# Independent work set between the steps of VectorE's dependent chains, two small steps given to ScalarE, and the two convolution tiles in turn

## The reference

```python
# block 1, a selective state-space layer (512 channels, 16 states)
xb, z = split(rms_norm(x) @ in_proj_w)            # 512 + 512
xc = silu(causal_depthwise_conv(xb, 4 taps) + conv_b)
dt, B, C = split(xc @ x_proj_w, [1, 17])
dt = softplus(dt @ dt_proj_w + dt_proj_b)
h_t = exp(dt_t * A) * h_(t-1) + dt_t * B_t * xc_t # for each channel and state
y_t = sum over states of h_t * C_t
y = (y + xc * D) * silu(z) @ out_proj_w + residual
# block 2, a mixture of 16 experts (256 -> 128 -> 256)
scores = sigmoid(x @ gate_weight.T)               # + e_bias for the choice only
# 2 of 4 groups by their two best scores, then the 4 best experts within them,
# weights = the chosen scores over their sum
y = sum over experts of weight * (silu(x @ Wg) * (x @ Wu)) @ Wd
```

## Time and profile before

| | |
|---|---|
| median of 3 runs | 2573.94 us (2572.68 to 2574.6) |
| the profiled execution | 2572.43 us, span 2570.6 us |
| busy of the span: PE, DVE, ACT, POOL | 92%, 92%, 62%, 58% |
| granted TensorE clock, mean | 0.971 |
| steady passes | 2 to 13, about 150 us each |

### The profile page before, as it was taken

One profiled execution on the slowest core, in us unless ns is written; L12 is line 12 of the kernel. 1 busy time (PEld: TensorE's weight loads), 2 busy tenths in 40 slices (PEclk: granted clock), 3 DMA queues, 4 the chain that ended last, 5 costly groups with the idle time before them and its releaser, 6 DMA issues.

```text
span 2570.6 us, 26578 instructions
## 1 busy us (share of the span) xinstructions
PE 2361.5 (92%) x8416; PEld 1172.0 (46%) x8416; DVE 2375.5 (92%) x2831; ACT 1602.5 (62%) x3186; POOL 1494.2 (58%) x531
## 2 busy tenths in 40 slices
PE   6556899999999999999999999999999999988998
PEld 2112354544545454454545445454544545443555
DVE  4989999999999999999999999999999999999642
ACT  6566567666766667676676667666666766654341
POOL 0555556657566665756666575656657566666522
PEclk9778899999999999999999999999999999998999
DMA  4442433535353453534344353534535353443232
GB/s 151 168 147 77 152 117 131 169 98 187 114 161 120 137 172 100 185 114 156 124 142 167 98 186 116 163 117 139 170 100 184 116 158 114 143 157 93 76 77 63
DMA packets 172919, 344.48 MB, mean 134 GB/s; under 512 B 16075, under 2 KB 81388, under 8 KB 164460
## 3 DMA queue, kind: packets, MB, share of 16 engines
q1 hardware_dynamic: 164860, 334.93, 39.0%
q0 software_dynamic: 7920, 7.87, 2.3%
HBM read 291.35 MB, written 51.38 MB: 133 GB/s over the span
## 4 chain that ended last, share of the span: by engine, by line
DVE 63%; issue 18%; PE 10%; ACT 8%; DMA 0%; POOL 0%; DVEq 0%; ACTq 0%; POOLq 0%
DVE hs L1085 30%; DVE hs L1065 14%; DVE th L1185 5%; DVE th L1180 5%; PE MY L511 2%; PE Gp L493 2%; PE Up L501 2%; DVE XC L1027 2%; ACT dA L604 1%; ACT SZ L677 1%; DVE SZ L1092 1%; ACT L604 1%; DVE DX L1049 1%; ACT L677 1%; PE FP L418 1%
## 5 line engine op out<-in xcount | busy, mean ns | idle before, releaser
L947 POOL TENSOR_TENSOR hs<-hs,Cb 128x2048 f32<-128x2048 f32 x256 | 1159.2, 4528 | 160.3 <-DVE hs L1065 159.7
L604 ACT ACTIVATE dA<-dtr,A 128x512 f32<-128x512 f32 x1024 | 700.8, 689 | 732.8 <-DVE hs L1085 730.3
L932 POOL TENSOR_TENSOR th<-th,cmb 128x512 f32<-128x512 f32 x256 | 325.8, 1275 | 899.5 <-DVE hs L1065 805.0
L1085 DVE TENSOR_TENSOR_SCAN hs<-dA,carry,hs 128x512 f32<-128x512 f32 x512 | 626.7, 1264 | 5.9 <-ACT dA L604 5.5
L1085 DVE TENSOR_TENSOR_SCAN hs<-dA,hs 128x512 f32<-128x512 f32 x512 | 595.0, 1202 | 14.2 <-ACT dA L604 13.7
L1065 DVE TENSOR_TENSOR hs<-dxr,Bb 128x2048 f32<-128x2048 f32 x255 | 586.1, 2298 | 1.6 <-PE Y L527 1.6
L493 PE MATMUL Gp<-x2T,Wgu 128*128 128x512 f32 x1024 | 510.5, 621 | 24.8 <-DVE th L1180 24.1
L511 PE MATMUL MY<-Wdn,th 128*128 128x256 f32 x2048 | 485.9, 381 | 0.8 <-POOL th L932 0.8
L501 PE MATMUL Up<-x2T,Wgu 128*128 128x512 f32 x1024 | 482.5, 593 | 0.0
L511 PEld LDWEIGHTS MY<-Wdn,th 128*128 128x128 f32 x2048 | 383.4, 190 | 136.2 <-issue 92.8
L493 PEld LDWEIGHTS Gp<-x2T,Wgu 128*128 128x128 f32 x1024 | 177.1, 191 | 353.4 <-issue 277.6
(11 more groups left out here) (180 smaller groups left out, 1754.0 us busy)
## 6 DMA issues: line engine op xcount, KB each, us to landing
dxr<-dx_d SPq DMA_DIRECT2D x128, 512.0 KB, 7.1
cmb<-cm_d SPq DMA_DIRECT2D x256, 256.0 KB, 3.6
dtr<-dt_d SPq DMA_DIRECT2D x63, 1024.0 KB, 5.5
Wdn<-in_w_dn SPq DMA_DIRECT2D x256, 128.0 KB, 3.4
Bb<-bc_d SPq DMA_DIRECT2D x64, 256.0 KB, 3.0
Cb<-bc_d SPq DMA_DIRECT2D x64, 256.0 KB, 3.4
dt_d<-XB SPq DMA_DIRECT2D x15, 1024.0 KB, 4.3
dx_d<-DX SPq DMA_DIRECT2D x15, 1024.0 KB, 5.8
```

The costliest lines, as they stand in the source:

```text
L604: act.activation(dA[h % 2][:, :], dtr[:, M % 2, beta, :], ACT.Exp, scale=A[:, k:k + 1]).then_inc(s_dA, 1)
L932: pool.tensor_tensor(th[:, q % NTH, :], th[:, q % NTH, :], cmb[:, q % 2, :], ALU.mult).then_inc(m_a, 1)
L947: pool.tensor_tensor(hs[:, G % NH, :, :], hs[:, G % NH, :, :], Cb[:, s, :].unsqueeze(1).broadcast_to([P, NBETA, CH]), ALU.mult).then_inc(s ...
L1085: dve.tensor_tensor_scan(hv, dA[h % 2][:, :], hv, first, ALU.mult, ALU.add).then_inc(s_h, 1)
```

## The change

Five things are changed.

1. `inputs` can be issued in parts, by 4 (512 columns each) or by 8 (256 columns each). In group 4 the four parts are set into `newton` of `norms`, after its steps guess, t0, y0 and t1; in group 6 likewise in `p_scale2`; in group 9 of passes with `R_` eight parts are set into the routing. The `inputs` at the end of these groups goes. `s_u` is raised by the last part, and the wait on `s_y` is before the first.
2. In group 9, `y_out` stands behind the routing's first instruction and no longer behind its last.
3. The variance of `p_scale2` (step `Bw1`) is now an activation of ScalarE (`var2`), and `comb` is now written by four activations of ScalarE (`p_comb`, behind `f_softplus` in group 9). The factor 0.5 moves into the copy `cmT`.
4. The two convolution tiles are both done in group 3, tap by tap in turn: tile 0, tile 1, tile 0, and so on; none is done in group 2.
5. In group 12 ScalarE issues `tanh` before two of the `decay` and not behind them.

```diff
@@ -184,12 +184,12 @@
             ['xT0', 'xT1', 'raw0', 'tap0', 'raw1', 'tap1', 'raw2', 'raw3', 'tap2', 'tap3', 'silu_x', 'z0', 'xd', 'dt', 'z1', 'z2', 'z3', 'silu_z'])
-        f_dve = Steps(sem('f_dve'), [f'c{k}{m}' for m in DVE_CONV for k in range(HIST)] + ['hist', 'dx'])
+        f_dve = Steps(sem('f_dve'), [f'c{k}{m}' for k in range(HIST) for m in DVE_CONV] + ['hist', 'dx'])
         fp_full = sem('fp_full')
         s_u, s_dA, s_h, s_keep, s_c, s_y, y_gate = (sem(k) for k in ('s_u', 's_dA', 's_h', 's_keep', 's_c', 's_y', 'y_gate'))
-        route = ['score', 'sfc', 'ps', 'hs', 'gs', 'geq', 'ggt', 'gq', 'gr', 'tmp', 'top', 'le', 'eq', 'nle', 'cs', 'ok', 'oke', 'sel', 'w', 'ws', 'wr', 'comb']
-        p_dve = Steps(sem('p_dve'), ['Bw1'] + rsqrt_names('q') + ['Bnb'] + route)
-        p_act = Steps(sem('p_act'), ['xn0', 'xn1', 'rev0', 'nm0', 'rev1', 'nm1', 'sq', 'ro', 'sq2', 'x2', 'x2T0', 'x2T1', 'ex', 'sig', 'cmT'])
+        route = ['score', 'sfc', 'ps', 'hs', 'gs', 'geq', 'ggt', 'gq', 'gr', 'tmp', 'top', 'le', 'eq', 'nle', 'cs', 'ok', 'oke', 'sel', 'w', 'ws', 'wr']
+        p_dve = Steps(sem('p_dve'), rsqrt_names('q') + ['Bnb'] + route)
+        p_act = Steps(sem('p_act'), ['xn0', 'xn1', 'rev0', 'nm0', 'rev1', 'nm1', 'sq', 'ro', 'sq2', 'var2', 'x2', 'x2T0', 'x2T1', 'ex', 'sig', 'comb', 'cmT'])
         m_g, m_u, m_d, m_th, m_v, m_w, m_a = (sem(k) for k in ('m_g', 'm_u', 'm_d', 'm_th', 'm_v', 'm_w', 'm_a'))
...
         z_dve = Steps(sem('z_dve'), ['w1'] + rsqrt_names('r') + ['nb'])
@@ -478,7 +478,7 @@
                 bank_free(p, 'ct')
-                pe.wait_ge(p_dve.sem, p_dve.at(c, 'comb'))
+                pe.wait_ge(p_act.sem, p_act.at(c, 'comb'))
                 for b in range(TB):
...
                 mm.then_inc(fp_full, 1)
@@ -729,6 +729,8 @@
                 squares(x1[:, (p - 1) % 2, :, :], b_s, n_nm[:, (p - 1) % 4, TB:2 * TB], dx_half).then_inc(p_act.sem, 1)
+                act.wait_ge(p_act.sem, p_act.at(p - 1, 'sq2'))
+                act.activation(p_w[:, 0, :], b_s[:, :], ACT.Copy, scale=1.0 / DM, bias=LN_EPS).then_inc(p_act.sem, 1)
 
...
                 c = p - 1
@@ -758,11 +760,20 @@
 
+            def p_comb(p):
+                c = p - 1
+                act.wait_ge(p_dve.sem, p_dve.at(c, 'wr'))
+                if c > 0:
+                    act.wait_ge(fp_full, filled(p - 1, 'ct'))
+                for b in range(TB):
+                    ins = act.activation(comb[:, b * NE:(b + 1) * NE], picked[:, b, 0:NE], ACT.Copy, scale=R[:, 7, 2 * TB + b:2 * TB + b + 1])
+                ins.then_inc(p_act.sem, 1)
+
             def p_cmT(p):
...
                     act.wait_ge(st_cm, 16 * (p - 1))
-                act.activation(cmT[:, :], FP[0:NE, :], ACT.Copy).then_inc(p_act.sem, 1)
+                act.activation(cmT[:, :], FP[0:NE, :], ACT.Copy, scale=0.5).then_inc(p_act.sem, 1)
 
...
                 p = c + 2
@@ -868,10 +879,12 @@
                     z_squares(p - 2)
+                if g == 12 and experts_at(G):
+                    tanh(experts_at(G)[0])
                 if 0 <= G + 1 < NGRP:
...
                     decay((G + 1) * NBETA + 1)
-                if experts_at(G):
+                if g != 12 and experts_at(G):
                     tanh(experts_at(G)[0])
...
                     keep_ends(G)
@@ -906,6 +919,8 @@
                     f_softplus(p)
+                if R_ and g == 9:
+                    p_comb(p)
                 if R_ and g == 10:
...
                 if F and g == 11:
@@ -975,22 +990,26 @@
 
-            def newton(steps, c, tag, v, y, a):
+            def newton(steps, c, tag, v, y, a, part=lambda k: None):
                 def done(name):
...
                 dve.tensor_scalar(y.bitcast(I32), v.bitcast(I32), -0.5, RSQRT_MAGIC, ALU.mult, ALU.add).then_inc(steps.sem, 1)
+                part(0)
                 done('guess')
...
                 dve.tensor_tensor(a, a, v, ALU.mult).then_inc(steps.sem, 1)
+                part(1)
                 done('t0')
...
                 dve.scalar_tensor_tensor(out=y, in0=a, scalar=1.875, in1=y, op0=ALU.add, op1=ALU.mult).then_inc(steps.sem, 1)
+                part(2)
                 done('y0')
...
                 dve.tensor_tensor(a, a, v, ALU.mult).then_inc(steps.sem, 1)
+                part(3)
                 done('t1')
...
                 done('y1')
@@ -1012,19 +1031,19 @@
                 dve.wait_ge(n_dve.sem, n_dve.at(i, 'var'))
-                newton(n_dve, i, 'r', n_v[:, c0:c1], n_rs[:, i % 4, c0:c1], n_a[:, c0:c1])
+                newton(n_dve, i, 'r', n_v[:, c0:c1], n_rs[:, i % 4, c0:c1], n_a[:, c0:c1], lambda k: inputs(p * GPC + 5, k, 4))
                 dve.tensor_tensor(n_nb[:, i % 4, c0:c1], n_nm[:, i % 4, c0:c1], n_rs[:, i % 4, c0:c1], ALU.mult).then_inc(n_dve.sem, 1)
 
-            def conv(p, m):
+            def conv(p):
                 c = p + 1
-                dve.wait_ge(f_act.sem, f_act.at(c, f'tap{m}'))
-                if m == DVE_CONV[0] and c > 0:
+                dve.wait_ge(f_act.sem, f_act.at(c, f'tap{DVE_CONV[-1]}'))
+                if c > 0:
                     dve.wait_ge(f_dve.sem, f_dve.at(c - 1, 'hist'))
-                xc = XC[:, c % 2, m, :]
                 for k in range(HIST):
-                    if k > 0:
-                        dve.wait_ge(f_dve.sem, f_dve.at(c, f'c{k - 1}{m}'))
-                    dve.scalar_tensor_tensor(out=xc, in0=XB[:, m, k:k + CH], scalar=conv_w[:, m, k:k + 1], in1=xc, op0=ALU.mult, op1=ALU.add).then_inc(f_dve.sem, 1)
+                    for m in DVE_CONV:
+                        if k > 0:
+                            dve.wait_ge(f_dve.sem, f_dve.at(c, f'c{k - 1}{m}'))
+                        dve.scalar_tensor_tensor(out=XC[:, c % 2, m, :], in0=XB[:, m, k:k + CH], scalar=conv_w[:, m, k:k + 1], in1=XC[:, c % 2, m, :], op0=ALU.mult, op1=ALU.add).then_inc(f_dve.sem, 1)
 
...
                 c = p + 1
@@ -1042,27 +1061,39 @@
                 if in_p(p):
-                    dve.wait_ge(p_dve.sem, p_dve.at(p - 1, 'comb'))
+                    dve.wait_ge(p_act.sem, p_act.at(p - 1, 'comb'))
                 if c == 0:
...
 
-            def inputs(G):
+            def inputs(G, k=0, parts=1):
+                if not 0 <= G < NGRP:
+                    return
                 c, M, s = (G // GPC, G // NSIG, G % NSIG)
...
                     return
-                if s == 0:
-                    for k in range(2):
-                        dve.wait_ge(ld_dx[2 * (M % 2) + k], 16 * (M // 2 + 1))
-                if M % MT == 0:
-                    dve.wait_ge(ld_B[s], 16 * (c + 1))
-                if G >= NH:
-                    dve.wait_ge(s_y, G - NH + 1)
-                dve.tensor_tensor(hs[:, G % NH, :, :], dxr[:, M % 2, :, :], Bb[:, s, :].unsqueeze(1).broadcast_to([P, NBETA, CH]), ALU.mult).then_inc(s_u, 1)
+                if k == 0:
+                    if s == 0:
+                        for half in range(2):
+                            dve.wait_ge(ld_dx[2 * (M % 2) + half], 16 * (M // 2 + 1))
+                    if M % MT == 0:
+                        dve.wait_ge(ld_B[s], 16 * (c + 1))
+                    if G >= NH:
+                        dve.wait_ge(s_y, G - NH + 1)
+                if parts <= NBETA:
+                    n = NBETA // parts
+                    u, dx_, B_ = (hs[:, G % NH, k * n:(k + 1) * n, :], dxr[:, M % 2, k * n:(k + 1) * n, :], Bb[:, s, :].unsqueeze(1).broadcast_to([P, n, CH]))
+                else:
+                    beta, half = divmod(k, 2)
+                    t = slice(half * CH // 2, (half + 1) * CH // 2)
+                    u, dx_, B_ = (hs[:, G % NH, beta, t], dxr[:, M % 2, beta, t], Bb[:, s, t])
+                ins = dve.tensor_tensor(u, dx_, B_, ALU.mult)
+                if k == parts - 1:
+                    ins.then_inc(s_u, 1)
 
...
                 c, h = (G // GPC, G * NBETA + beta)
@@ -1093,10 +1124,8 @@
                 c = p - 1
-                dve.wait_ge(p_act.sem, p_act.at(c, 'sq2'))
-                variance(p_w[:, 0, :], b_s[:, :]).then_inc(p_dve.sem, 1)
-                dve.wait_ge(p_dve.sem, p_dve.at(c, 'Bw1'))
-                newton(p_dve, c, 'q', p_w[:, 0, :], p_w[:, 1, :], p_w[:, 2, :])
+                dve.wait_ge(p_act.sem, p_act.at(c, 'var2'))
+                newton(p_dve, c, 'q', p_w[:, 0, :], p_w[:, 1, :], p_w[:, 2, :], lambda k: inputs(p * GPC + 7, k, 4))
                 dve.tensor_tensor(p_nb[:, :], n_nm[:, c % 4, TB:2 * TB], p_w[:, 1, :], ALU.mult).then_inc(p_dve.sem, 1)
...
             den, score, sfc, tmp, eq, le, cs = (R[:, k, :] for k in range(7))
@@ -1124,6 +1153,8 @@
                 dve.reciprocal(score, den).then_inc(p_dve.sem, 1)
+                if 0 <= p < NC:
+                    y_out(p * GPC + 7)
                 done('score')
...
                 done('sfc')
@@ -1131,6 +1162,7 @@
                 dve.tensor_tensor(trip[:, :, 2], hi[:, :, 0], hi[:, :, 1], ALU.add).then_inc(p_dve.sem, 1)
+                inputs(p * GPC + 10, 0, 8)
```

(19 more changed lines are left out.)

## The result

The changed kernel takes 2580.54 us (median of 8 runs, 2576.08 to 2582.3), the kernel before 2572.74 (8 runs beside it, 2567.65 to 2574.6). The ratio is 1.0033, with a 95% interval of 1.0024 to 1.0042. The forecast of 2548 was wrong by 32.5 us and in its sign. The profiled execution took 2582.03 us, span 2580.2, granted clock 0.969.

What follows compares the result with a forecast made beforehand. VectorE leads, with TensorE's list a second bound over two thirds of a pass; seven even passes (8.5), six odd (13.3) and passes 0, 1, 15, 16 together gain 26.2 us, giving 2548 us, range 2538 to 2562.

Steps and rivals of the forecast that it cites:

- Group 4: four of nine links are broken, 0.48, three more instructions, 0.18: 0.30 us: VectorE's `norms` chain in group 4: weaving in four product parts saves 0.30 us a pass.
- Group 6: the same 0.30: VectorE's `p_scale2` chain in group 6: weaving saves 0.30 us, with the variance's 0.20 together 0.50 us a pass.
- A link is worth 0.12 us, a part costs 0.06.: VectorE unit prices: breaking a link between dependent instructions saves 0.12 us; each additional product part costs 0.06 us.
- the two groups of the convolution: Groups 2 and 3 on VectorE: taking the tiles in turn removes four links, 0.48 us a pass, nothing added.
- a link is worth nothing: Rival at every broken link: worth under 0.02 us, so 6.6 us more, 2580.5; chance 4%.
- The variance saves 0.20 us, behind a delay by the scan.: Group 6: variance leaves VectorE, 0.20 us saved; 0.11 of its 0.31 step is a delay behind a scan.
- Group 9 gives 0.99 us.: Routing: nine broken links 1.08 us, `comb` and its link 0.33, seven more instructions cost 0.42; sum 0.99 us.
- Routing to gate: Sign of being right: first routing reciprocal to the gate of group 10 takes 7.5 us instead of 8.51.
- TensorE lets 1.22 us through in even passes, 2.21 in odd ones.: Of VectorE's 2.27 us a pass, waits for TensorE's results leave 1.22 us in even passes, 2.21 in odd.
- `p_comb` takes 0.8 to 0.9 us and hides the table load by half a microsecond.: ScalarE before group 10's third scan: four activations take 0.8 to 0.9 us, hidden, since up to 1.36 fits.
- The sum.: All passes together gain 26.2 us, from the profiled 2572.43 to 2546.2; run median 2547.7, rounded 2548.
- something else: Remainder beside the forecast and its named rivals, with no place or size given; chance 3%.

Runs made afterwards that it cites:

- the first experiment: Changed kernel plus two waits on GpSimd, so it starts its multiplication only behind the chain's last instruction (`nb`) in groups 4 and 6: 2546.37 us, 0.9894.
- the run without parts: Changed kernel with the product in groups 4 and 6 whole again, behind `nb` at the end of these groups: 2551.33 us, 0.9913.
- the last version: Changed kernel with GpSimd waiting for `nb`, plus `y_out` of group 5 behind `add_x1` and `e_norm` in group 9 ahead of `f_softplus`: 2544.05 us, 0.9886.

## Why the prediction was wrong

It was wrong at one place. The step that failed is in the part by part costs, "Group 4: four of nine links are broken, 0.48, three more instructions, 0.18: 0.30 us" and "Group 6: the same 0.30 [...] together 0.50 us". Both price an instruction by its kind, its size and its link, and nothing by what another engine does in that moment. I checked whose result each moved instruction waits for, and did not ask what the end of the product sets going. It raises `s_u`, GpSimd starts 0.08 us after that end, and the last small step of both chains now comes 0.13 us after it. Start of the first scan of a group to that of the next, against the kernel before, in steady passes: group 4 costs 0.80 us instead of giving 0.30, group 6 0.60 instead of giving 0.50. That is 2.2 us a pass against the forecast. Passes 0 and 1 pay 3.9, 3.9 and 3.7 us where `read_out` is met.

A sign of it stood in the trace of before, where I did not look. In the tail, VectorE's `add_x1` (two inputs in SBUF) takes 1.76 us, against 1.22 in the earlier trace rows, and ends where GpSimd's instruction leaves it room:

```profile
2454.51 1.76 DVE L1198 TENSOR_TENSOR x<-DX,x 128x1024 f32<-128x1024 f32 x1 [0.66 <-ACT DX L737]
...
2453.92 1.27 POOL L932 TENSOR_TENSOR th<-th,cmb 128x512 f32<-128x512 f32 x1 [7.30 <-DVE th L1185]
```

GpSimd ends at 2455.19; what is left of VectorE's is 1.08 us, close to the 1.13 of its undisturbed step in the earlier trace rows. In the passes the kernel before hides most of it. GpSimd's two instructions behind a product last together 5.8 us, and for nearly that long VectorE has the gate, the scans and `up`, each with an operand in PSUM; that `nb` stood ahead of the product was part of this cover.

A second sign is the 0.28 us of the first small instruction in the earlier trace rows, which the prediction put down to the scan ahead of it. It ends at 1283.19, GpSimd's `read_out` at 1283.16. The same instruction in pass 9, behind a scan as well, comes when `read_out` has just ended (1428.30 + 4.53 = 1432.83) and takes half of that:

```profile
1432.83 0.14 DVE L999 TENSOR_SCALAR p_w<-b_s 128x4 f32<-128x4 f32 x1
...
1428.30 4.53 POOL L947 TENSOR_TENSOR hs<-hs,Cb 128x2048 f32<-128x2048 f32 x1
```

It is so in all passes from 2 to 15: 0.28 or 0.29 us in the even ones, 0.14 in the odd. So the scan was not the cause. The kernel before already met GpSimd there, and in more places. In each even pass seven products follow a scan directly, start 0.24 us before `read_out` ends and take 2.38 to 2.41 us; in odd passes such a product starts at its end and takes 2.26. That the scans of odd passes are others is not the reason: in the changed kernel the product at 1302.42, in group 7 of the even pass 8, comes 1.15 us after the end of `read_out` and takes 2.27. VectorE's product and the `read_out` beside it in group 7 of pass 8:

```profile
1292.78 2.39 DVE L1065 TENSOR_TENSOR hs<-dxr,Bb 128x2048 f32<-128x2048 f32 x1
...
1288.50 4.53 POOL L947 TENSOR_TENSOR hs<-hs,Cb 128x2048 f32<-128x2048 f32 x1
```

It also sets one sentence ahead of the prediction right, that the engines meet only through semaphores: here two of them met with none between them.

The Trainium skill has the rule. Its page "SBUF — State Buffer", section "Who interferes with whom", says that a VectorE instruction with two SBUF inputs contends with a GpSimd instruction that reads SBUF, and one in a mode that uses both ports with GpSimd too; the two share a port pair, whoever starts first has it for its whole length, and the other is blocked entirely. The runs agree as far as they go: 0.17 us for the VectorE instruction that starts first, 1.26 and 4.49 for the one that starts 0.03 to 0.05 us second. No run here shows the reverse, GpSimd held by VectorE. It also lists the multiplication by a scalar among the operations that can take both ports, and the 1.26 us of the one-input form agree with that. I weighed another of its rules in the prediction, where this one was the rival to name.

The other steps, by the first experiment, in which the collision alone is taken out (2546.4 measured, 2547.7 forecast for exactly that mechanism):

- *A link is worth 0.12 us, a part costs 0.06.* Right. Parts step by 0.60 us (1272.02 to 1272.62). Group 4 of odd passes gives 0.30, group 6 0.49, the two groups of the convolution 0.49; forecast 0.30, 0.50, 0.48. The rival "a link is worth nothing" is refuted, though the measured time stands beside its 2580.5: the two agree by chance. The rule of the Trainium skill behind it ("VectorE: DVE Perf Modes", "The DRAIN you can't avoid") does not hold here for instructions of 4 to 128 columns (0.20 us linked against 0.08 on 4 columns), nor for the 512 of the convolution, where four links less gave 0.49.
- *The variance saves 0.20 us, behind a delay by the scan.* The size is right (0.19 to 0.22 in group 6 of the run without parts), the reason was not: the delay is GpSimd's, see above.
- *Group 9 gives 0.99 us.* Slightly more: 1.10 in the changed kernel, 1.08 in the first experiment. Routing to gate takes 7.43 us instead of 8.51, forecast 7.5.

```profile
1318.28 0.52 DVE L1155 RECIPROCAL DX<-DX 128x64 f32<-128x64 f32 x1
1318.72 0.62 DVE L1123 TENSOR_TENSOR SZ<-Y,SZ 128x512 f32<-128x512 f32 x1
...
1325.62 0.17 DVE L1211 RECIPROCAL DX<-DX 128x4 f32<-128x4 f32 x1
1325.71 0.65 DVE L1215 SCALAR_TENSOR_TENSOR th<-th,Gp 128x512 f32<-128x512 f32 x1
```

- *TensorE lets 1.22 us through in even passes, 2.21 in odd ones.* Right: 1.2 and 2.4. Group 5 of even passes takes back 0.74 in the first experiment (0.68 of it the wait for `Y`). Group 9 gives 0.82 there, since a wait for `dA` begins to show (11.6 us in 19 times, 10.8 in 13 in the changed kernel).
- *`p_comb` takes 0.8 to 0.9 us and hides the table load by half a microsecond.* Right: 0.91, and the scan of group 10 does not wait. ScalarE of the changed kernel:

```profile
1325.83 0.91 ACT L769 ACTIVATE comb<-picked,DX 128x16 f32<-128x16 f32 x4 [1.76 <-DVE DX L1211]
1326.76 1.28 ACT L604 ACT_TABLE_LOAD   x1
1328.05 0.69 ACT L604 ACTIVATE dA<-dtr,A 128x512 f32<-128x512 f32 x1
```

- *The sum.* The terms held; one was missing, put at nothing without a look at it, and with more than their total: 43.6 us of VectorE's time, 34.2 in the time of the whole. As "something else" it had 3%. The reading of what bounds the kernel was not at fault: VectorE led, and so what it lost before group 9 of each pass, beyond TensorE's slack, was seen in the end.

What stays open: by how much the last version is faster than the first experiment's, and why a reciprocal is not held; the runs show that it is not, and nothing on the reason.

## What to carry to other kernels

Before an instruction is moved past one that raises a semaphore, ask what that semaphore starts on GpSimd, and what VectorE does while it runs: one small instruction with two operands in SBUF, or a multiplication of one, then lasts until GpSimd's ends, whatever its size. Put the small ones ahead of the instruction that releases GpSimd, or let it wait for them; that delayed GpSimd by 0.36 us here and gave 34 us. And read mean durations by form after each change: lost time of this kind stands in the busy column, and no list of waits shows it.

## What the runs showed of the hardware

- A VectorE instruction on 4 to 16 columns that starts 0.03 to 0.05 us behind a GpSimd multiplication of SBUF tiles takes 1.25 to 1.28 us (GpSimd's 1.26 to 1.29) or 4.49 to 4.50 (GpSimd's 4.50 to 4.51). One that starts 0.16 us ahead takes 0.17 and is through when GpSimd begins.
- A VectorE product of 2048 columns that starts 0.24 us before the end of GpSimd's `read_out` takes 2.38 to 2.41 us, one that starts at that end 2.26.
- Held means that the instruction lasts until GpSimd's ends. Held were a `TENSOR_TENSOR` of two SBUF tiles and a `TENSOR_SCALAR` of one. A `RECIPROCAL` of one was not (0.18 to 0.25 us).
- 3.06 us without work on TensorE were followed by a granted clock of 0.53, and four matmuls took 3.59 us instead of 1.88.
- Four activations of 16 columns with a scale operand take 0.91 us together, little more than the 0.20 each of 64 columns without one.
